# A pre-norm transformer layer on one core: block ends, a tile's place, a layout in memory and the order of the last products

## The chip, the cores and the metric

One core of one Trainium2 chip computes the whole layer in one launch. The metric is the device time of that launch in microseconds. The kernel before was timed three times: 2402.41, 2403.76 and 2404.12 us; the median is 2403.76 us.

## The reference

The input `x` is 2 sequences of 2048 tokens with 1024 features, all in float32. `_layernorm` without gamma and beta is applied ahead of each half.

```python
x = x + attn(layernorm(x))        # one head: d = 256, Wqkv 1024 x 768, Wo 256 x 1024, biases
    # softmax(q k^T / 16) v, then Wo and bo
x = x + ffn(layernorm(x))
    # logits = h @ gate_w (8 experts); s = sum of the two largest logits
    # shared = relu(h @ up_w) ** 2 @ down_w             (1024 -> 2048 -> 1024)
    # routed = ((h @ fc1_w) @ expert_w * s) @ fc2_w     (1024 -> 512 -> 512 -> 1024)
    # layernorm(shared + routed) * ln_gamma + ln_beta
```

The whole routed branch is linear but for the factor `s`, so `expert_w @ fc2_w` (called e2) is formed once, and up with fc1 and down with e2 are two products of inner width 2560.

## The kernel before

**Precision.** Each float32 operand is split into a high part (ScalarE, `A`, line 99) and a low part (VectorE, `TT`, line 102), and each product is three TensorE products (`mm`, line 114): high x high, high x low, low x high.

**Queues.** Every engine runs its instructions in the order in which the program appended them. A wait belongs to the instruction ahead of which it stands, and all behind it on that engine wait as well. DMAs are issued by SP or, for most stores, by ScalarE's queue (`q=act`), and wait there in order too. The order is written out by hand. A `Plan` holds tasks under a number: `plan.add(n, task)` appends what `plan.run(n)` emits behind the products of step n.

**Stage 1, opening.** e2 is computed, x's first tile of 512 tokens is normalised (`ln_stats`, `ln_rstd`, `ln_norm`; the reciprocal root runs on GpSimd) and transposed by TensorE (`xt_tr`) out of `RAW` and split (`xt_evac`).

**Stage 2, q, k and v.** Eight tiles t of 12 steps: eight half groups of q and k, four groups of v. `ev_qk_f` (ScalarE) and `ev_v_f` (VectorE) take the results out of PSUM into a ring of three slots `OUT`; each waits until the slot's last store has landed. Beside it the weights of the FFN are combined, split and stored (`quad_tasks`).

**Stage 3, attention.** Eight blocks i of 512 queries with eight steps k: scores of block i+1 (`pe_S`), product with v of block i (`pe_PV`), and on the other engines subtraction, exponential, high part, sum and low part (`P_sub`, `P_exp`, `P_h`, `P_acc`, `P_l`). At a block's end: `row_sums(i)`, `pe_S(i + 2, 0)`, then `m_tr` (transpose of the running maximum, after `m_fold`), a reduction to `m` on VectorE, `m_bc` (broadcast), and twelve groups `pe_wo` of six products of OH and OL with Wo, whose results `ev_wo` (ScalarE) writes into `ATT` and stores to `att_s`. `pe_wo` used banks 4, 5, 6, 7 in turn.

**LN2.** `ln2_tasks(t, tt)` makes one tile of 128 tokens of the second layernorm: loads, sum to x1, statistics, gate logits, store of x1 + beta (`x1b_s`), normalisation, a transpose in 32 x 32 blocks on VectorE (line 977) and, with the fourth tile, the store of 512 tokens to `xT_s` by 16 DMAs in pieces of 512 B. x1's tiles of t = 1 stood at FFN steps -1, 2, 5 and 8.

**Stage 4, FFN.** Four passes s over 1024 tokens. Both products use a seven-product scheme over 2 x 2 quarters. Up: seven products p in the order 1, 2, 6, 7, 4, 5, 3, ten chunks each; a chunk is 12 products of 512 columns; its moving operand is one of seven combinations B11, B21, T2, T3, T4, T1, B22 of transposed x1, made by `x_sum` and split by `x_piece` into halves. Down: the same order, ten steps each (`d_chunk`, with ring slots filled by `h_op`), results added into quarters A, B (`ZR0`) and D, C (`ZR1`) by `z_evac`; then `z_stat`, `z_fin`, `z_out` and `z_store` make the last layernorm and the residual. A chunk's weights (512 KB) are loaded ahead by `w_fill` from `wu_s` or `wd_s` into six buffers `WR`. Chunks 0 to 6 stand between the steps of the last attention block, chunks 7 to 12 in and ahead of its output groups. In the tail after the last pass, product 3 is done tile by tile and finishes A and B.

Of the kernel before, what the change touches and what calls it, by code (L numbers as in the profile page):

```python
# [69 lines left out]
def transformer_layer(nc, x, wqk, wv, bqk, bv, wo, woT, bo, boc, gate, upfc, dn, expT, fc2, gamma, beta, out):  # L70
# [69 lines left out]
    xT_s = nc.dram_tensor("xT_s", (8, 128, 4096), F32).ap()  # L140
# [249 lines left out]
    ln_norm(0, 1)  # L390
    ln_stats(0, 3)
    ln_rstd(0, 3, 4)
    e2_mm(3, 0)
    f_split(0, 1)
# [6 lines left out]
    f_split(2, 1)  # L401
    xt_tr(0, 0)
# [4 lines left out]
    e2_mm(1, 1)  # L407
# [3 lines left out]
    e2_mm(2, 1)  # L411
# [18 lines left out]
    def out_slot():  # L430
        s = out_n[0] % 3
        out_n[0] += 1
        return s
# [9 lines left out]
    def ev_qk_f(t, i):  # L443
        s = out_slot()
        ev_qk[t, i] = A(OUT[:, s, :], bank(i % 2), AF.Identity, t_pqk[t, i], ld_bq, *out_tok.get(s, ()), bias=bqs[:, i:i + 1])
        out_at[t, i] = s

    def st_qk_f(t, i):
        s = out_at[t, i]
        st_qk[t, i] = dma(qk_s[t, i], OUT[:, s, :], f"out{s}", ev_qk[t, i], q=act)  # L450
        out_tok[s] = (st_qk[t, i],)
# [33 lines left out]
    def kv_load(b, what, k):  # L485
# [8 lines left out]
        else:  # L494
# [3 lines left out]
                                *stg["free"].get(s, ()))  # L498
# [27 lines left out]
    def pe_S(i, k, *toks0):  # L526
        h, lo = QA[i % 2]
        b = i // 4
        for c in range(2):
# [171 lines left out]
    for a in range(4):  # L701
        plan.add(4 + a // 2, xt_tr, 1, a)
        plan.add(4 + a // 2, lambda a=a: xt_evac(1, a, wsp[4], st_e2[0])())
# [60 lines left out]
    T2 = at("T2", [128, 32, 4, 32], F32, 204.71875)  # L764
# [74 lines left out]
    def pe_PV(i, k):  # L839
        b = i // 4  # L840
        h, lo = pslot(i, k)
        for d in range(2):
            o = bank(4 + d)
            for c in range(2):
                kt = 2 * k + c
                toks = [pl_t[i, k], kv_sp[b, "v", k]]
                if k == 0 and i > 0:
                    toks += [att_ev[i - 1, 9]]
# [36 lines left out]

    def pe_wo(i, g):

        tt, c = divmod(g, 3)
        o = bank(4 + g % 4, 344)
# [3 lines left out]
        elif g == 3:  # L893
            prev = rinv_t[i]
        else:
            prev = att_ev[i - 1, 10] if i else wg[1]
        toks = [o_t[i], wo_sp[1], prev]
        for d in range(2):
            mm(o, OH[:, d, ts_], WOH[:, d, ns], d == 0, False, *toks)
            mm(o, OH[:, d, ts_], WOL[:, d, ns], False, False)  # L900
            wo_pe[i, g] = mm(o, OL[:, d, ts_], WOH[:, d, ns], False, d == 1, sig=(d == 1))

    def ev_wo(i, g):
# [5 lines left out]
        att_ev[i, g] = A(ATT[:, n % 2, 344 * c:344 * c + 344], bank(4 + g % 4, 344), AF.Copy, *toks, scale=rinv[:, tt:tt + 1])  # L909
# [774 lines left out]
```

How the kernel before makes its waits and increments, by code:

```python
    def wait(self, *toks):  # L43
        for sem, val in toks:
            if self.known.get(sem.name, 0) < val:
                self.known[sem.name] = val
                self.ops.append(lambda e, s=sem, v=val: e.wait_ge(s, v))
# [1 line left out]
    def put(self, fn, *toks, sig=True):  # L49
        self.wait(*toks)
        if not sig:
            self.ops.append(fn)
            return None
        self.count += 1
        self.ops.append(lambda e: fn(e).then_inc(self.sem, 1))
        return (self.sem, self.count)
# [34 lines left out]
    def dma(dst, src, sl, *toks, q=None):  # L91
        s = slot(sl)
        s.n += 16
        (q or sp).wait(*toks)
        (q or sp).ops.append(lambda e: e.dma_start(dst, src).then_inc(s.sem, 16))
        return (s.sem, s.n)
```

## Time and profile before

| | before |
|---|---|
| median of three runs | 2403.76 us |
| profiled execution | 2404.65 us, its span 2402.8 us |
| TensorE busy | 2330.0 us, 97% of the span, 10888 products |
| VectorE busy | 1577.0 us, 66% |
| ScalarE busy | 790.2 us, 33% |
| GpSimd busy | 284.1 us, 12% |
| mean granted TensorE clock | 0.988 |

A product counts as busy from its start to its modelled end, and one starts before the one ahead has ended; so the pace is read from the number of products in a stretch. PE is TensorE's products, PEld its weight loads, DVE VectorE, ACT ScalarE, POOL GpSimd; SPq and ACTq are the queues that issue DMAs. The times of all rows are microseconds from the span's start unless marked ns.

### The profile page before, as it was taken

How to read it: one execution, taken by the hardware profiler on the slowest of the kernel's cores; microseconds unless marked ns; L12 is line 12 of the kernel's file. 1: busy time of each engine (PE TensorE's matmuls, PEld its weight loads, DVE VectorE, ACT ScalarE, POOL GpSimd, SP SyncE). 2: the span in 40 equal slices, each digit the busy share in tenths (PEclk: the TensorE clock that was granted, in tenths of full speed). 3: DMA queues.
4: the chain of work that ended last, by engine and by line, in shares of the span. 5: the costliest groups of instructions: out<-in, count | busy, mean ns of one | idle time of the engine just before them, and what ended most of it. 6: DMA issues, size and time to landing. Idle time of an engine off the chain costs nothing. (4 is left out here: it accounts for less than half of the span.)

```text
span 2402.8 us, 27319 instructions
## 1 busy us (share of the span) xinstructions
PE 2330.0 (97%) x10888; PEld 1951.2 (81%) x10888; DVE 1577.0 (66%) x1758; ACT 790.2 (33%) x875; POOL 284.1 (12%) x574
## 2 busy tenths in 40 slices
PE   8999999999999889999999999999999999999997
PEld 7989887878888667888888888888888888888885
DVE  7777538888888746478774259876238876434537
ACT  4343325666655432331213132213132121223110
POOL 2101000000031210023210013210003221000002
PEclk9999999999999899999999999999999999999998
DMA  7899624445434587888997678998667999666676
GB/s 292 315 335 363 221 69 137 155 161 193 154 112 135 206 298 252 291 302 288 320 343 240 194 238 272 349 325 280 193 219 266 309 320 330 208 192 195 194 222 201
DMA packets 256895, 581.87 MB, mean 242 GB/s; under 512 B 27520, under 2 KB 114176, under 8 KB 254336
## 3 DMA queue, kind: packets, MB, share of 16 engines
q1 hardware_dynamic: 175392, 444.57, 56.7%
q10 hardware_dynamic: 81376, 135.55, 15.2%
q8 instruction: 86, 1.41, 0.2%
q14 instruction: 41, 0.34, 0.0%
HBM read 424.58 MB, written 155.45 MB: 241 GB/s over the span
## 5 line engine op out<-in xcount | busy, mean ns | idle before, releaser
L102 DVE TENSOR_TENSOR HB<-HB,psum 128x1024 f32<-128x1024 f32 x140 | 169.0, 1217 | 294.1 <-PE psum L114 294.1
L99 ACT ACTIVATE HB<-HB 128x1024 f32<-128x1024 f32 x128 | 135.8, 1061 | 345.4 <-DVE HB L102 343.4
L114 PE MATMUL psum<-XS2h,WR 128*128 128x512 f32 x560 | 176.6, 394 | 13.6 <-issue 10.7
L105 POOL TENSOR_SCALAR veA<-mvA 128x1 f32<-128x1 f32 x32 | 31.1, 971 | 1338.2 <-DVE mvA L191 1338.2
L114 PE MATMUL psum<-XS1h,WR 128*128 128x512 f32 x560 | 176.2, 392 | 3.0 <-DMA WR<-wu_s 3.0
L114 PE MATMUL psum<-XS0h,WR 128*128 128x512 f32 x560 | 175.3, 389 | 0.0
L114 PE MATMUL psum<-XS3h,WR 128*128 128x512 f32 x560 | 174.1, 389 | 0.0
L114 PEld LDWEIGHTS psum<-XS2h,WR 128*128 128x128 f32 x560 | 106.5, 190 | 36.9 <-issue 11.1
L114 PEld LDWEIGHTS psum<-XS1h,WR 128*128 128x128 f32 x560 | 106.0, 189 | 25.9 <-DMA WR<-wu_s 3.8
L114 PEld LDWEIGHTS psum<-XS0h,WR 128*128 128x128 f32 x560 | 105.3, 188 | 21.8
L114 PEld LDWEIGHTS psum<-XS3h,WR 128*128 128x128 f32 x560 | 105.1, 188 | 21.8
L114 PE MATMUL psum<-XS2l,WR 128*128 128x512 f32 x280 | 110.1, 393 | 0.0
L114 PE MATMUL psum<-XS1l,WR 128*128 128x512 f32 x280 | 109.7, 392 | 0.0
L114 PE MATMUL psum<-XS0l,WR 128*128 128x512 f32 x280 | 108.9, 389 | 0.0
L114 PE MATMUL psum<-XS3l,WR 128*128 128x512 f32 x280 | 108.9, 389 | 0.0
L114 PE MATMUL psum<-PH,VH 128*128 128x512 f32 x256 | 101.7, 397 | 3.4 <-DVE PL L102 3.1
L114 PE MATMUL psum<-PL,VH 128*128 128x512 f32 x256 | 100.7, 393 | 0.0
L114 PE MATMUL psum<-PH,VL 128*128 128x512 f32 x256 | 100.6, 393 | 0.0
L102 DVE TENSOR_TENSOR PL<-SA,PH 128x1024 fp32r<-128x1024 f32 x64 | 78.0, 1219 | 29.1 <-ACT PH L99 29.1
L114 PE MATMUL psum<-WR,RG20h 128*128 128x512 f32 x288 | 89.0, 390 | 2.1 <-DMA WR<-wd_s 2.1
L114 PE MATMUL psum<-WR,RG30h 128*128 128x512 f32 x288 | 88.7, 389 | 0.5 <-DMA WR<-wd_s 0.5
L114 PE MATMUL psum<-WR,RG00h 128*128 128x512 f32 x288 | 88.7, 389 | 0.0
(308 smaller groups left out, 5903.4 us busy)
## 6 DMA issues: line engine op xcount, KB each, us to landing
WR<-wu_s SPq DMA_DIRECT2D x280, 512.0 KB, 4.4
WR<-wd_s SPq DMA_DIRECT2D x280, 512.0 KB, 4.8
att_s<-ATT ACTq DMA_DIRECT2D x32, 516.0 KB, 3.0
RAW<-in_x_dram SPq DMA_DIRECT2D x32, 512.0 KB, 8.0
RES<-x1b_s SPq DMA_DIRECT2D x128, 128.0 KB, 5.0
wd_s<-QHc ACTq DMA_DIRECT2D x18, 896.0 KB, 4.8
wd_s<-QRc ACTq DMA_DIRECT2D x18, 896.0 KB, 4.6
HB<-xT_s SPq DMA_DIRECT2D x14, 1024.0 KB, 8.6
```

The source lines that it names most:

```text
L99: return act.put(lambda e: e.activation(o, i, f, **kw), *toks)
L102: return (q or dve).put(lambda e: e.tensor_tensor(o, a, b, op=op), *toks)
L105: return (q or dve).put(lambda e: e.tensor_scalar(o, a, s1, s2, op0=op0, op1=op1), *toks)
L114: return pe.put(lambda e: e.matmul(o, w, m, start=start, stop=stop, **kw), *toks, sig=sig)
```

## The change

The opening's statements are reordered; the transposes of x's second tile stand at plan numbers 5 to 8; the OUT ring has five slots for the first five tiles. At block ends half of the next scores goes behind `m_tr`, `pe_wo` does its OL products last and uses banks 6, 4, 5, 7. Tile (1, 0) of LN2 is begun in block 6; the other three of t = 1 start at 0, 4 and 8; `x_load`, `x_sum` and the pieces that depend on them are two numbers earlier; fewer weight loads are issued in block 6; `row_sums(7)` stands later. `xT_s` has a new layout: a tile is stored by 4 DMAs in pieces of 4 KB, loaded in pieces of 2 KB, and one product reads its 512 columns as four runs of 128. In the last pass the down products run in the order 1, 2, 6, 5, 3, 7, 4, so that A and B are complete first, and the tail finishes C and D.

```diff
@@ opening
+    e2_mm(3, 0)
+    f_split(0, 1)
     ln_stats(0, 3)
     ln_rstd(0, 3, 4)
-    e2_mm(3, 0)
-    f_split(0, 1)
...
     e2_mm(0, 1)
     f_split(2, 1)
+    e2_mm(1, 1)
     xt_tr(0, 0)
...
     f_split(3, 1)
-    e2_mm(1, 1)
+    e2_mm(2, 1)
     wq_split(0)
     xt_tr(0, 2)
     xt_evac(0, 2)()
-    e2_mm(2, 1)
@@ ring
+    outs = [OUT[:, 0, :], OUT[:, 1, :], OUT[:, 2, :], STG[:, 0, :], STG[:, 1, :]]
+
+    def out_slot(t):
+        s = out_n[0] % (5 if t < 5 else 3)
...
     for a in range(4):
-        plan.add(4 + a // 2, xt_tr, 1, a)
+        plan.add(5 + a, xt_tr, 1, a)
@@ block ends
+    def wo_bank(g):
+        return (6, 4, 5, 7)[g % 4]
...
         for d in range(2):
-            mm(o, OH[:, d, ts_], WOH[:, d, ns], d == 0, False, *toks)
+            mm(o, OH[:, d, ts_], WOH[:, d, ns], d == 0, False, oh_t[i], wo_sp[1], prev)
             mm(o, OH[:, d, ts_], WOL[:, d, ns], False, False)
-            wo_pe[i, g] = mm(o, OL[:, d, ts_], WOH[:, d, ns], False, d == 1, sig=(d == 1))
+        for d in range(2):
+            wo_pe[i, g] = mm(o, OL[:, d, ts_], WOH[:, d, ns], False, d == 1, o_t[i], sig=(d == 1))
...
                 if i + 2 < 8:
-                    pe_S(i + 2, 0)
+                    pe_S(i + 2, 0, cs=(0,))
                 m_tr(i + 1)
+                if i + 2 < 8:
+                    pe_S(i + 2, 0, cs=(1,))
                 m_bc(i + 1, sub_t[i, 7])
@@ layout of x1's transposed copy
-    T2 = at("T2", [128, 32, 4, 32], F32, 204.71875)
+    T2 = at("T2", [128, 4, 8, 4, 32], F32, 204.71875)
...
             if tt == 3:
-                for m in range(4):
-                    src = T2[32 * g:32 * g + 32].rearrange("p (j m) t r -> p m j (t r)", m=4)[:, m]
-                    to = xT_s[t, 32 * m:32 * m + 32].rearrange("c (j g q) -> c g j q", g=4, q=128)[:, g]
-                    xt_st[t] = dma(to, src, "xt", ln2_tr[t, 3])
+                src = T2[32 * g:32 * g + 32].rearrange("p m k t r -> p m (k t r)")
+                xt_st[t] = dma(xT_s[t, g].rearrange("(m c) n -> c m n", m=4), src, "xt", ln2_tr[t, 3])
...
-        src = xT_s[2 * s + c, :, 2048 * r:2048 * r + 2048].rearrange("p (j n) -> p j n", j=4)
+        src = xT_s[2 * s + c, :, :, 512 * r:512 * r + 512].rearrange("g p n -> p g n")
...
-            mm(o, w[:, 0, ws], x[0][:, kt, :], kt == 0, False, *toks)
+            mm(o, w[:, 0, ws], x[0][:, :, ws], kt == 0, False, *toks)
@@ attention's end
+    ffn_plan = Plan()
+    x1_tile = ln2_tasks(1, 0, LX, LA, BO, T2, (BETA_A, ld_beta_a), (0, 3))
+    for n, task in zip((53, 53, 61, 61, 61, 61, 65, 65), x1_tile):
+        plan.add(n, task)
+    for n, task in zip((-1, -1, -1, 0), x1_tile[8:12]):
+        ffn_plan.add(n, task)
...
             if i == 6 and g == 0:
                 x_load(0, 0, 0, S_pe_end)
                 x_load(0, 0, 1, S_pe_end)
-                w_fill(0)
-            if i == 6 and g >= 8:
-                x_piece(0, ("B11", "B21")[g // 2 - 4], g % 2)
+            if i == 6 and g == 4:
+                w_fill(-3)
+            if i == 6 and g in (8, 10):
+                x_piece(0, "B11", g // 2 - 4)
+            if i == 6:
+                plan.run(56 + g)
...
-            for tt in range(4):
+            plan.add(-1, w_fill, -1)
+            for tt in range(1, 4):
                 def run(tt=tt):
-                    ln2_at(plan, 3 * tt - 1, LN2_U0, 1, tt, LX, LA, BO, T2, (BETA_A, ld_beta_a), divmod(3 + tt, 4))
-                plan.add(3 * tt - 1, run)
+                    ln2_at(plan, 4 * tt - 4, LN2_U0[tt - 1], 1, tt, LX, LA, BO, T2, (BETA_A, ld_beta_a), (1, tt - 1))
+                plan.add(4 * tt - 4, run)
+            for h in range(2):
+                plan.add(2 + h, x_piece, 0, "B21", h)
...
-                plan.add(14, x_load, 0, 1, r, lambda: (pv_t[7, 7],))
+                plan.add(12, x_load, 0, 1, r, lambda: (pv_t[7, 7],))
...
-                plan.add(16 + n // 2, x_sum, s, name, h)
+                plan.add(14 + n // 2, x_sum, s, name, h)
...
-        if k == 6:
-            row_sums(7)
-            row_inv(7)
     o_evac_h(7)
     o_evac_l(7)
-    for _ in range(2):
-        chunk(nup)
-        nup += 1
+    chunk(nup)
+    row_sums(7)
+    row_inv(7)
+    chunk(nup + 1)
+    nup += 2
@@ last pass
+    PRODS = [(1, 2, 6, 7, 4, 5, 3)] * 3 + [(1, 2, 6, 5, 3, 7, 4)]
...
+        elif s == 3 and p == 6:
+            t = TT(ZD, ZB, src, ALU.add, k, *zt("B"), *free(1))
+            done("D", t)
+        elif s == 3 and p == 5:
+            t = TT(ZC, ZD, src, ALU.add, k, *zt("D"), *free(1))
+            done("C", t)
+        elif s == 3 and p == 3:
+            t = TT(ZB, ZC, src, ALU.add, k, *zt("C"))
+            done("B", t)
+        elif s == 3 and p == 7:
+            done("C", TT(ZC, ZC, src, ALU.add, k, *zt("C")))
+            t = TT(ZD, ZD, src, ALU.add, k, *zt("D"))
+            done("D", t)
...
+    RES = [at(f"RES{i}", [128, 2, 512], F32, o) for i, o in enumerate((168, 172, 0, 4, 8, 12, 16, 20))]
...
+        if s == 3:
+            for tt in range(4):
+                for r in range(2):
+                    plan.add(d + 4 + 8 * tt + 4 * r, lambda r=r, tt=tt: res_load(3, r, tt, up_pe[3, 3, 9]))
+                plan.add(d + 42 + tt, z_stat, 3, 0, tt, 0)
+                plan.add(d + 50 + tt // 2, z_stat, 3, 0, tt, 1)
+                plan.add(d + 52 + 2 * tt, z_out, 3, 0, tt)
+                plan.add(d + 53 + 2 * tt, z_store, 3, 0, tt)
+            plan.add(d + 51, z_fin, 3, 0, 0, 4)
```

## Rows read from the trace of the kernel before

**Rows 1.** The page, section 1: busy us, share of the span, instructions of each engine

```profile
PE 2330.0 (97%) x10888; PEld 1951.2 (81%) x10888; DVE 1577.0 (66%) x1758; ACT 790.2 (33%) x875; POOL 284.1 (12%) x574
```

**Rows 2.** TensorE's waits in the whole run: in total, times, longest

```profile
PE psum L353 <- DVE RAW L105: 8.2, 6, 3.8
PE psum L575 <- DVE m L569: 5.5, 7, 0.8
PE psum L114 <- ACT ATT L99: 4.6, 2, 4.3
PE psum L568 <- DVE mx L102: 3.9, 3, 2.8
PE psum L871 <- DVE acc L102: 3.9, 1, 3.9
PE psum L114 <- DVE OL L102: 3.3, 7, 0.5
PE psum L114 <- DVE PL L102: 3.1, 4, 1.1
PE psum L114 <- DMA WR<-wu_s: 3.0, 2, 2.1
PE psum L114 <- DVE XS2l L102: 2.9, 1, 2.9
PE psum L114 <- DVE F2L L102: 1.9, 2, 1.2
```

**Rows 3.** Stretches: length, busy us (instructions) of each engine, PEclk, DMA share, GB/s

```profile
0.00:60.00 60.00, 52.60 (x254) 43.76 (x255) 42.98 (x66) 26.37 (x34) 17.30 (x50) 0.97 0.80 292
140.00:165.00 25.00, 20.79 (x132) 18.84 (x131) 14.80 (x23) 8.00 (x10) 3.03 (x7) 0.93 0.93 334
780.00:840.00 60.00, 50.04 (x201) 40.13 (x200) 48.21 (x53) 24.32 (x27) 13.99 (x29) 0.89 0.57 212
880.00:910.00 30.00, 14.35 (x46) 10.43 (x46) 21.70 (x22) 5.97 (x7) 0.00 (x0) 0.76 0.61 238
1200.00:1260.00 60.00, 60.00 (x266) 49.56 (x265) 47.83 (x54) 11.01 (x11) 8.51 (x12) 1.00 1.02 344
```

**Rows 4.** VectorE's timeline at 156 us: start, us, engine, line, operation, idle before

```profile
156.61 0.43 DVE L102 TENSOR_TENSOR OUT<-psum,bvb 128x264 f32<-128x264 f32 x1 [5.81 <-DMA qk_s<-OUT]
```

**Rows 5.** Timeline at the end of block 4, VectorE and TensorE

```profile
650.57 0.64 DVE L102 TENSOR_TENSOR mx<-mx 128x512 f32<-128x512 f32 x1
652.68 0.60 PE L568 MATMUL psum<-idn,mx 128*128 128x128 f32 x4
655.19 0.42 PE L114 MATMUL psum<-WOH,OH 128*128 128x344 f32 x1 [0.48 <-DVE OL L102]
```

**Rows 6.** Timeline ahead of the last block, ScalarE and SP's queue

```profile
784.50 0.99 ACT L99 ACTIVATE ATT<-psum,rinv 128x344 f32<-128x344 f32 x2 [4.99 <-DMA att_s<-ATT]
775.62 4.24 SPq L95 DMA_DIRECT2D WR<-wu_s  x5
```

**Rows 7.** Timeline of x1's second half: VectorE, SP's queue, VectorE, TensorE

```profile
859.53 1.25 DVE L977 STREAM_TRANSPOSE T<-LX 128x1024 f32<-128x1024 f32 x1
867.43 7.56 SPq L95 DMA_DIRECT2D xT_s<-T  x8
888.10 1.23 DVE L102 TENSOR_TENSOR HB<-HB,XS0h 128x1024 f32<-128x1024 f32 x1 [10.48 <-DMA HB<-xT_s]
902.41 0.77 PE L114 MATMUL psum<-XS2h,WR 128*128 128x512 f32 x1 [10.71 <-issue]
```

**Rows 8.** Timeline of the tail, TensorE and VectorE

```profile
2385.40 0.39 PE L114 MATMUL psum<-WR,RG30l 128*128 128x512 f32 x1
2380.49 0.67 DVE L102 TENSOR_TENSOR ZR<-ZR,psum 128x512 f32<-128x512 f32 x1
2391.99 0.68 DVE L102 TENSOR_TENSOR ZR<-ZR,psum 128x512 f32<-128x512 f32 x1
2396.94 1.42 DVE L108 SCALAR_TENSOR_TENSOR ZR<-ZR,rZ,RES 128x512 f32<-128x512 f32 x2 [0.69 <-DVE ZR L108]
```

More of the change, by code:

```diff
@@ L443, in ev_qk_f @@
     def ev_qk_f(t, i):
[L444 to L445 removed]
+        s = out_slot(t)
+        ev_qk[t, i] = A(outs[s], bank(i % 2), AF.Identity, t_pqk[t, i], ld_bq, *out_tok.get(s, ()), bias=bqs[:, i:i + 1])
         out_at[t, i] = s
@@ L449, in st_qk_f @@
         s = out_at[t, i]
-        st_qk[t, i] = dma(qk_s[t, i], OUT[:, s, :], f"out{s}", ev_qk[t, i], q=act)
+        st_qk[t, i] = dma(qk_s[t, i], outs[s], f"out{s}", ev_qk[t, i], q=act)
         out_tok[s] = (st_qk[t, i],)
@@ L524, in transformer_layer, with pe_S @@
     MB_t, mxf = {}, {}
-    def pe_S(i, k, *toks0):
+    def pe_S(i, k, *toks0, cs=(0, 1)):
         h, lo = QA[i % 2]
         b = i // 4
-        for c in range(2):
+        for c in cs:
             kt, bk = 2 * k + c, 2 * (k % 2) + c
@@ L1571, in transformer_layer @@
         if g == 11:
-            bank_free.update({4 + b: (att_ev[7, 8 + b],) for b in range(4)})
+            bank_free.update({wo_bank(n): (att_ev[7, n],) for n in range(8, 12)})
         if g % 3 == 2:
@@ L1589, in transformer_layer, with tail_out1, tail_out2 @@
     for tt in range(4):
-        res_load(3, 0, tt)
-    for tt in range(4):
-        z_stat(3, 0, tt, 0)
+        z_stat(3, 1, tt, 1)
     mul = {}
-    def tail_out1(tt):
-        for c in range(2):
-            z, cs = ZR[0][:, c, tt, :], slice(512 * c, 512 * c + 512)
-            mul[tt] = STT(z, z, mvZ[:, tt, 0:1], GAMMA[:, cs], ALU.subtract, ALU.mult, ag_t[3, 0, tt])
-    def tail_out2(tt):
-        for c in range(2):
-            z, cs = ZR[0][:, c, tt, :], slice(512 * c, 512 * c + 512)
-            k = STT(z, z, rZ[:, tt:tt + 1], RES[tt][:, c, :], ALU.mult, ALU.add, mul[tt], fin[3, 0, tt], res_ld[3, 0, tt])
-            for ps, rs in parts(3, 0, tt):
-                dma(out[rs, cs], ZR[0][ps, c, tt, :], f"zo{tt}{c}", k, q=(act, sp)[c])
+    def tail_out1(tt, c):
+        z, cs = ZR[1][:, c, tt, :], slice(512 * c, 512 * c + 512)
+        mul[tt] = STT(z, z, mvZ[:, tt, 0:1], GAMMA[:, cs], ALU.subtract, ALU.mult, ag_t[3, 1, tt])
+    def tail_out2(tt, c):
+        z, cs = ZR[1][:, c, tt, :], slice(512 * c, 512 * c + 512)
+        k = STT(z, z, rZ[:, tt:tt + 1], RES[4 + tt][:, c, :], ALU.mult, ALU.add, mul[tt], fin[3, 1, tt], res_ld[3, 1, tt])
+        for ps, rs in parts(3, 1, tt):
+            dma(out[rs, cs], ZR[1][ps, c, tt, :], f"zo{tt}{c}", k, q=(act, sp)[c])
     done = {}
```

127 lines of the change are left out of this document (63 added, 64 removed).

## The prediction

> **What bounds the kernel now.** I began with the page's busy shares: TensorE is busy 97% of the span [rows 1], and no part of the change takes away a matrix product. So the change can only take away time in which TensorE stands or runs slowly. I looked for that time in two views: TensorE's waits over the whole run [rows 2], and stretches of time with TensorE's count of products and its granted clock [rows 3]. The last row of rows 3 gives the pace when nothing is in the way: 266 products of 512 columns in 60 us, 0.226 us each. The others show what is lost. From 880 to 910 us only 46 products start, 10.4 us of work in 30 us: 19.6 us are lost in one place. From 780 to 840 the mean clock is 0.89; 0.11 below full is 0.22 of the 60 us at 1.2 instead of 2.4 GHz, 13 us that do half their work: 6.6 us lost beside the waits. The same arithmetic gives 3.6 us at 1.2 GHz (1.8 us lost) in 0 to 60 and 3.5 us (1.7 lost) in 140 to 165. The waits of rows 2, the late start of the second x1 half and the end of the run are the whole field: about 80 us, most of it between 780 and 910 us, where the attention ends and the FFN begins.
>
> The profiled execution lasted 2404.65 us (span 2402.8). The sum below is made against 2404.65; the median of the runs is 0.9 us less.
>
> **1. Opening: orders of a few statements.** `f_split(0, 1)` now stands ahead of the statistics of tile 3, so TensorE's 1.2 us for F2L goes (the larger of two, 1.9 in all [rows 2]). `e2_mm(1, 1)` ahead of the first transposes puts 12 products (2.7 us) before the wait for the normalised RAW, but that normalisation gets 0.7 us later. The transposes of tile row 1 move one to three chunks later (plan 4, 4, 5, 5 to 5, 6, 7, 8), behind 2.7 us of products. RAW costs 8.2 us in all, of which 3.8 belong to part 2; of the other 4.4 I take 2.8, and half of the 1.8 us of clock: 1.2 + 2.8 + 0.9 = 4.9 us. What is late next: `pe_v(0, 2)` waits for the evacuation of the last transpose with one product group of cover; I price that at nothing and keep 1 us in the range.
>
> **2. OUT ring of five.** At 156.6 VectorE waited 5.81 us for a store of `qk_s` before it could reuse an OUT slot [rows 4]. Queued behind it are two normalisations, and TensorE's transposes wait for those: 3.8 us, the longest wait for RAW, and 1.7 us of clock [rows 2, 3]. With five slots for t < 5 the slot in question was stored two evacuations earlier. The two extra slots are the staging buffers, first loaded for other use at plan 67, behind the last stores. Gain 5.5 us.
>
> **3. Block ends.** At seven ends TensorE transposes the running maximum, waits 0.8 for its reduction (m), broadcasts it, and waits 0.5 for OL (5.5 and 3.3 us over seven [rows 2]). Now half of the next scores (6 products, 1.36 us) stands between the transpose and the broadcast, and the first output group does its four OH products before it needs OL; its bank order 6, 4, 5, 7 lets it start while banks 4 and 5 are still read. From the transpose to the output product it took 655.19 - 652.68 = 2.51 us [rows 5]; two groups of four small transposes (0.44 each, as far as the second starts behind the first, an estimate from their 0.60) and the moved 1.36 make 2.24, of which 1.36 is work that was elsewhere: 0.88 against 2.51, 1.6 us saved. That needs the folded maximum 1.36 us sooner. At 652.68 it had been ready since 651.21, 1.47 us before: enough, and this is the smallest slack of four ends (the others have 1.8 to 3.0). At two ends TensorE was waiting for the fold (mx) itself (three waits, 3.9 us, the longest 2.8 [rows 2]; the third is ahead of the first block); there the moved half only lengthens that wait, and 0.3 us is left (2.51 less 2.24). The last end has no next scores: only OL, 0.5. Sum 4 x 1.6 + 2 x 0.3 + 0.5 = 7.5 us. VectorE's own work per block doesn't shrink, so I subtract 0.5 for P parts that come later relative to TensorE: 7.0.
>
> **4. Before the last block.** ScalarE waited 4.99 us for `att_s<-ATT`, TensorE 4.3 of the 4.6 for ATT [rows 2, 6]. The store was in flight together with 2 MB of x1 and five 512 KB weight loads issued from 775.6 [rows 6]. Now there are two of those, and the x1 loads are issued earlier: 4 issues instead of 16 write x1's transposed copy ahead of them. The wait goes; of the 6.6 us of clock [rows 3] half hangs on it, the other half on part 5. 4.3 + 3.3 = 7.6, less 1.2 because `x_piece` and the early tile now stand in ScalarE's and VectorE's queues there: 6.4 us.
>
> **5. Last block.** `row_sums(7)` goes behind `o_evac_l(7)` and one more chunk, 8 us later: the 3.9 us for acc and its 3.3 us of clock go, 7.0 us, since the inverse is needed only at output group 3, after another chunk. Against it: LN2 tile (1, 0) is added in the output products of block 6, and tiles 1 to 3 follow every 4 chunks. I laid VectorE's queue beside TensorE's, at 1.2 us per operation of 1024 elements [rows 7]: 17 operations for the block's subtractions, sums and low parts, 2 for the end of tile (1, 0), 6.5 for each of two tiles, 2 for B21, 34 operations or 41 us. TensorE has 15 groups of 12 products, 41 us: no slack. PL waits were 3.1 us [rows 2]; I expect about 1 us more. Net 6.0.
>
> **6. x1's second half.** The chain of before: the last LN2 tile is transposed at 859.5 to 860.8; SP issues the copy in 16 transfers (eight of them from 867.43, ending at 875.0); VectorE gets B12 at 888.1 after 10.48 us of idling; TensorE starts product 6 at 902.4 after 10.71 us [rows 7], then waits 2.9 more [rows 2]. 27.3 us from transpose to data, 14.3 from data to product. TensorE was ready at 902.4 - 10.7 = 891.7, and without the weight wait of 2.1 [rows 2] and 1.7 us of clock just before it would have been at 887.9. Now: the transpose comes about 1 us earlier relative to chunk 8 (its `att_s` load still waits for the store of the tile before it). The 2 MB copy, at the 344 GB/s of a full stretch [rows 3], is 6 us, with issue and landing 8; the load is at plan 12 instead of 14, so ahead of gamma's and beta's loads: 1 MB is 3.0 us at the same rate, with the 4.4 us that the last output took to land [rows 8] about 7. So 15 instead of 27.3 us: data at 859.8 + 15 = 874.8. VectorE reaches the sums, now at plan 14, at chunk 14's end, five chunks (13.6 us) before product 6 is due: 874.3. The 14.3 us stay: sums T1, T2, T4 and the first piece, all on VectorE in the same order. Product 6 has its data at 889.1, 1.2 us late. I take 1.5 us, the 2.9 for XS2l's second half unchanged and 2 us of clock: 6.4 of the 19.6 us stay, 13.2 go.
>
> Per group of four tiles SP spends 16 issues on the copy, eight of them 7.56 us [rows 7]; I lean on the issues, not on the piece size. The Trainium skill's page DMA: Bandwidth & Descriptors, section Specifications, sets the smallest transfer for line rate at 512 B; by that rule the larger pieces buy no transfer time. That result is rival B below. No run here shows the rule by itself.
>
> Reads of x1 now come in 2 KB instead of 8 KB pieces. Bounds: nothing, or another 3.0 us for a load of 1 MB; only the two of part 6 are without cover.
>
> **7. x1 as moving operand.** 280 chunks x 12 = 3360 products now read 512 columns as four runs of 128, a kind of read that no row shows. Below: 0 (a gain is excluded, since 0.226 us is also the pace with contiguous columns). Above: four transposes of 128 columns take 0.60 us [rows 5] against 0.226, +0.37 us each, some 1200 us. I take 0, the row with the same number of columns per instruction. The splits read strips of 256 with the same element count: 0 as well.
>
> **8. The end.** Before, TensorE ended at 2385.79, but VectorE began the first of four last tiles only at 2380.5, being busy with the other half's outputs; the last tile took from 2391.99 to 2398.36, 6.4 us, and everything was over 4.4 us later [rows 8]. With the order 1, 2, 6, 5, 3, 7, 4 the half A, B is complete two products earlier and its outputs lie beside products. A tile takes TensorE 18 products, 4.1 us, and VectorE 17.9 / 4 = 4.5 with its waits: it keeps up. The last tile then starts at about 2385.9 and ends at 2392.3: 6.1 us saved. The eight RES loads, 32 issues in four groups, pass SP with the weight loads: 0 to 1 us of weight wait.
>
> **Sum:** 4.9 + 5.5 + 7.0 + 6.4 + 6.0 + 13.2 + 6.1 = 49.1 us. 2404.65 - 49.1 = 2355.6; against the median 2354.7.
>
> **Rivals.**
> A. VectorE becomes the bound around the last block: it loses an operation's length or two at each of eight steps (8 x 1.2 us), the tiles slip, and with them part 6 by the same amount up to 5. For it: the balance of part 5 has no slack. Against: before, with two tiles, PL cost 3.1 us in all. 2355 + 10 + 3 = 2368.
> B. The copy of x1 isn't ready sooner: the landing, not the issues, set 875 to 888, and the larger pieces change no transfer. Then only the 2 chunks of earlier load (5.4 us) help and product 6 still waits about 5 us more, with its clock: 2355 + 7 = 2362.
> C. Better: block ends and B12 come out whole, the clock stays up: 1.5 + 2 + 1.2 + 1.8 us: 2348.
> D. Slower than before: the four-run read of part 7. It decides from 49.1 / 3360 = 0.015 us per product, 7% of the pace; at a tenth of the upper bound, 0.037, it is +124 us: 2479. Nothing in the profile speaks for it but that no row excludes it.
>
> **How the numbers follow.** Forecast 0.57, A 0.18, B 0.12, C 0.09, D 0.04. The time is the forecast's, 2354.7. The range takes in C and A and their bounds: 2342 to 2374. A measurement of this kernel can tell about 0.2% (5 us) from no change. Faster: all but D and a stray 0.02: 0.94; same 0.02; slower 0.04.
>
> **What would show it.** The page's chunks: 266 products in 60 us must stay (D). The wait for ATT and for acc absent (4, 5). m and OL absent at five ends, and the fold's wait longer at block 2 (3). VectorE's wait for `qk_s<-OUT` at 150 to 157 gone (2). Product 6 starts with under 3 us of wait; if B12's wait on VectorE is still 5 us or more, B. PL waits above 6 us would be A. The last output on VectorE ends 6 to 7 us after TensorE's last product, not 12.6 (8). The forecast is wrong if the 780 to 910 stretch gives back less than 15 us.

## The result, and the profile after

| | before | after |
|---|---|---|
| median | 2403.09 us (4 runs) | 2361.09 us (4 runs, 2359.59 to 2363.95) |
| profiled execution | 2404.65 us, span 2402.8 | 2361.47 us, span 2359.7 |
| mean granted TensorE clock | 0.988 | 0.994 |
| TensorE busy | 2330.0 us | 2318.3 us |

The ratio is 0.9826, 95% interval 0.9809 to 0.9843: 42 us gained, where 49.1 were forecast (2354.7 us; 2361.09 is inside the range). The spans differ by 43.1 us. The first part of the page of after answers to [rows 1]:

```profile
span 2359.7 us, 27222 instructions
PE 2318.3 (98%) x10888; PEld 1945.5 (82%) x10888; DVE 1576.2 (67%) x1758; ACT 788.8 (33%) x875; POOL 291.8 (12%) x574
```

TensorE's largest waits of after stand against [rows 2] (in total, times, longest):

```profile
PE psum L114 <- ACT ATT L99: 7.7, 7, 2.2
PE psum L570 <- DVE mx L102: 6.3, 4, 4.1
PE psum L114 <- DMA WR<-wu_s: 5.4, 3, 3.7
PE psum L114 <- DVE XS2l L102: 3.4, 1, 3.4
PE psum L114 <- DVE XA1l L102: 1.2, 1, 1.2
PE psum L114 <- DMA WR<-wd_s: 1.0, 1, 1.0
PE psum L114 <- DVE F2L L102: 0.9, 1, 0.9
PE psum L577 <- DVE m L571: 0.8, 1, 0.8
PE psum L114 <- DVE PL L102: 0.6, 1, 0.6
```

The waits for RAW (8.2), acc (3.9) and OL (3.3) are gone, m fell from 5.5 to 0.8, PL from 3.1 to 0.6. Three of those of before grew: ATT from 4.6 to 7.7, mx from 3.9 to 6.3, weights from 3.0 to 5.4. The same kinds of stretches as in [rows 3], moved to where the work now stands (columns as there):

```profile
0.00:60.00 60.00, 57.58 (x287) 48.40 (x288) 46.42 (x72) 26.80 (x34) 18.66 (x54) 1.00 0.81 301
140.00:165.00 25.00, 25.00 (x141) 21.69 (x140) 16.65 (x26) 8.39 (x10) 0.00 (x0) 1.00 1.05 399
745.00:805.00 60.00, 54.89 (x268) 46.74 (x268) 53.16 (x58) 31.03 (x38) 18.33 (x26) 1.00 0.73 250
845.00:875.00 30.00, 22.94 (x81) 17.89 (x81) 23.11 (x20) 9.54 (x10) 0.00 (x0) 0.80 0.76 274
1200.00:1260.00 60.00, 60.00 (x268) 49.67 (x268) 40.45 (x40) 21.92 (x22) 4.68 (x6) 1.00 0.91 294
```

The last row is the pace: 268 products in 60 us against 266. The two rows hold different products (161 of the 266 are down products, which read no x1), so the stronger evidence is one stretch of equal work: from the first to the last up product of the second pass it takes 191.11 us in before and in after. Four runs of 128 columns cost nothing. Three stretches are at full clock now. The row of 845 to 875 shows what is left: 81 products in 30 us, at a mean clock of 0.80.

I followed the gain by the start of the same product in both traces, as the timelines give it (us; the last column is what the stretch brought):

| product | before | after | in this stretch |
|---|---|---|---|
| first scores (parts 1, 2) | 327.72 | 316.46 | 11.25 |
| first output product of block 6 (part 3) | 771.08 | 752.72 | 7.10 |
| chunk 0 (part 4) | 794.85 | 774.57 | 1.92 |
| chunk 7 (part 5) | 840.28 | 809.93 | 10.07 |
| chunk 17 | 879.27 | 850.83 | -1.91 |
| chunk 21 (part 6) | 910.03 | 873.33 | 8.25 |
| last product | 2385.40 | 2347.68 | 1.03 |
| from there to the end | 17.4 | 12.0 | 5.4 |

These are single executions, and two things in them move from one to the next. Two kernels below whose opening is that of before start the first scores at 325.91 and 329.57 us. And in the 22 us around the end of block 5 the mean granted clock was 0.92 in before, in last_order_alone and in no_4k_layout, and 1.00 in ring_alone, in block_ends_alone and in after, which is worth about 2 us. So a difference of under 2 us between two traces is no proof, unless a wait in them shows it.

### The profile page after: what moved, and what is told of

The parts are those of the page before. It is cut to its first block, busy times and chain, and to the rows that moved or that the text cites. A ratio compares the mean times of both kernels' runs of the same rounds, so it can differ in the third digit from the quotient of the medians.

```text
span 2359.7 us, 27222 instructions
## 1 busy us (share of the span) xinstructions
PE 2318.3 (98%) x10888; PEld 1945.5 (82%) x10888; DVE 1576.2 (67%) x1758; ACT 788.8 (33%) x875; POOL 291.8 (12%) x574
## 4 chain that ended last, share of the span: by engine, by line
PE 81%; DVE 7%; DMA 7%; ACT 3%; issue 1%; POOL 1%; SPq 0%; ACTq 0%; DVEq 0%; POOLq 0%
PE psum L114 80%; DMA wu_s<-QR0a 2%; DMA QR0a<-in_upfc_dram 1%; DMA wd_s<-QRc 1%; DVE mx L102 1%; PE psum L353 1%; ACT SA L99 1%; DVE QR0a L102 1%; DVE HB L102 1%; DVE QRc L102 1%; DMA att_s<-ATT 1%; DVE acc L102 1%; ACT ATT L99 1%; DVE st L188 1%; DMA WR<-wu_s 1%
## 5 line engine op out<-in xcount | busy, mean ns | idle before, releaser
L114 PE MATMUL psum<-WR,RG10h 128*128 128x512 f32 x288 | 88.7, 389 | 0.0
```

The lines of the kernel that those rows point to most:

```text
L114: return pe.put(lambda e: e.matmul(o, w, m, start=start, stop=stop, **kw), *toks, sig=sig)
```

## Experiments

Each time is a median of one study's runs. Chips and hours move the kernel before from 2399.8 to 2404.2 us, so between studies the ratios to it are compared, and inside a trace the starts of products. Diffs are excerpts; `...` stands for lines left out.

**ring_alone.** The kernel before with the ring of five slots alone:

```diff
-    def out_slot():
-        s = out_n[0] % 3
+    outs = [OUT[:, 0, :], OUT[:, 1, :], OUT[:, 2, :], STG[:, 0, :], STG[:, 1, :]]
+
+    def out_slot(t):
+        s = out_n[0] % (5 if t < 5 else 3)
...
```

> The kernel before with the OUT ring of five alone. Theory (store wait): the 5.8 us wait of VectorE for a qk_s store at 150 to 157 us goes and with it TensorE's 3.8 us wait for RAW and 1.7 us of clock: 5 to 6 us less, and nothing else moves. Rival (the opening and the ring share the gain of 9.3 us that the changed kernel has at the first scores beyond the 2.0 of the opening): the ring alone gives clearly more or less than 5.5, outside 4.5 to 6.5.

2394.68 us, ratio 0.9971 (0.9961 to 0.9981): 7 us, above the 5 to 6 expected; the interval reaches down to 4.6. The first scores start 5.4 us sooner, and VectorE's wait for `qk_s<-OUT` of [rows 4] is gone. The trace's other 1.5 us lie at the end of block 5, where this trace has no dip of the clock; the ring has no part in that. Part 2 holds.

**last_order_alone.** The kernel before with the last pass in the new order and with the new tail:

```diff
-    SEQ_D = [(p, kt) for p in (1, 2, 6, 7, 4, 5, 3) for kt in range(10)]
+    PRODS = [(1, 2, 6, 7, 4, 5, 3)] * 3 + [(1, 2, 6, 5, 3, 7, 4)]
+    SEQ_D = [[(p, kt) for p in PRODS[s] for kt in range(10)] for s in range(4)]
...
```

> The kernel before with the last pass's order of down products, its eight RES buffers and the new tail alone. Theory: TensorE's end stays within 1 us, the last output follows TensorE's last product by 6 to 7 us instead of 12.6: 5 to 6.5 us less. Rival: the changed kernel gained another 1.6 us inside the last pass before the tail; if that belongs to this part (fewer weight waits there), the whole is 6.5 to 7.5 us less.

2396.72 us, ratio 0.9981 (0.9971 to 0.9990): 4.6 us, just under the 5 to 6.5 expected, which the interval covers. From the last product to the end it takes 11.6 us instead of 17.4. Part 8 holds.

**block_ends_alone.** The kernel before with the split scores, OL last and the bank order:

```diff
                 if k == 0 and i > 0:
-                    toks += [att_ev[i - 1, 9]]
+                    toks += [att_ev[i - 1, 10]]
...
+    def wo_bank(g):
+        return (6, 4, 5, 7)[g % 4]
...
-                    pe_S(i + 2, 0)
+                    pe_S(i + 2, 0, cs=(0,))
                 m_tr(i + 1)
+                if i + 2 < 8:
+                    pe_S(i + 2, 0, cs=(1,))
...
```

> The kernel before with the block ends alone (half of the scores behind the transpose of the maximum, OL products last, banks 6 4 5 7). Theory: 1.6 us less at the ends of blocks 0, 1, 3, 4, about 0.3 at 2 and 5, 0.5 at 6: 7 us less. Rival (as the changed kernel showed at block 2, where it lost 1.5 us): an end where the fold is late costs time, since the halved clock that follows the longer idle falls on products: 5 us less in all, with block 2 at +1 or worse.

2391.53 us, ratio 0.9957 (0.9941 to 0.9973): 10.3 us, where 7 were expected; the interval covers that. Block 6's first output product starts 9.9 us sooner, but 1.8 of these are there at the first scores already, which this edit does not touch: 8.1 belong to the blocks. By the output products, time is lost at block 2 alone (1.06 us): TensorE waits there for the fold, as in after. Two waits for ScalarE's evictions are new in this kernel, and in after too; before has none at these places:

```profile
779.48 0.76 PE L114 MATMUL psum<-PH,VH 128*128 128x512 f32 x1 [2.13 <-ACT ATT L99]
853.01 0.47 PE L114 MATMUL psum<-XS1h,WR 128*128 128x512 f32 x1 [1.17 <-ACT ATT L99]
```

**no_4k_layout.** The changed kernel with the old layout of `xT_s` (16 stores in pieces of 512 B, one contiguous moving operand), all else as changed:

```diff
-                src = T2[32 * g:32 * g + 32].rearrange("p m k t r -> p m (k t r)")
-                xt_st[t] = dma(xT_s[t, g].rearrange("(m c) n -> c m n", m=4), src, "xt", ln2_tr[t, 3])
+                for m in range(4):
+                    src = T2[32 * g:32 * g + 32].rearrange("p (j m) t r -> p m j (t r)", m=4)[:, m]
+                    to = xT_s[t, 32 * m:32 * m + 32].rearrange("c (j g q) -> c g j q", g=4, q=128)[:, g]
+                    xt_st[t] = dma(to, src, "xt", ln2_tr[t, 3])
...
```

> The changed kernel with the layout of x1's transposed copy undone: 16 stores per four tiles in 512 B pieces, loads in 8 KB pieces, moving operands contiguous. Theory of the prediction (issues set the copy's time): the copy of the second half takes 5 us longer or more, product 6 is later by as much: +5 to +10 us. Rival (the copy's rate is set by something that both layouts share; before, copy and load took 16.7 us to landing, now 14): only about 3 us at that place, +1 to +4 us in all. If reading four runs of 128 cost TensorE anything, this kernel would be faster than that by it; expected 0.

2368.56 us, ratio 0.9861 (0.9841 to 0.9881): by the ratios the layout is worth 8.4 us of the 42; the two intervals just overlap. The traces differ by 8.7 us, and only 2.3 of these lie between chunk 17 and chunk 21, where the layout was to help. Another 2.4 lie between block 6's first output product and chunk 0, where TensorE waits once, 5.34 us, in place of twice, 2.23 and 2.10; about 2 are the clock at the end of block 5. Two lines of SP's queue, first of no_4k_layout, then of after (start, duration of the issues):

```profile
834.52 13.61 SPq L95 DMA_DIRECT2D xT_s<-T  x16
850.50 0.80 SPq L95 DMA_DIRECT2D HB<-xT_s  x2
```

```profile
830.66 4.47 SPq L95 DMA_DIRECT2D xT_s<-T  x4
844.61 0.93 SPq L95 DMA_DIRECT2D HB<-xT_s  x2
```

The issues shrank by 9.1 us, but the time from the first issue to the load, which waits for the landing, only from 16.0 to 14.0 us. Over that time the DMA engines moved 245 GB/s in pieces of 512 B and 249 in pieces of 4 KB. The up products of the second pass take the same 191.11 us in both.

**no_copy_wait.** The changed kernel; in the first pass x1's second half is loaded from the copy of t = 0, which landed long ago. The sums work on other data, the rest is the same.

```diff
+        t = 0 if s == 0 else 2 * s + c
+        src = xT_s[t, :, :, 512 * r:512 * r + 512].rearrange("g p n -> p g n")
+        x_ld[s, c, r] = dma(raw, src, f"x{c}{r}", xt_st[t], *free())
```

> The changed kernel, with x1's second half of the first pass loaded from the copy of the first half (t = 0), which landed long ago; so the first pass works on other numbers there, and nothing waits for the copy of t = 1. Theory (the copy's 14 us to landing holds SP's queue, so weights, and the sums): the loads issue 7 us or more earlier, weight wait 3.7 goes, sums start at chunk 14's end, product 6 starts 6 to 8 us earlier; the 3.4 for the second half of XS2l stays. Rival (the sums' own length binds): product 6 at most 2 us earlier.

2363.16 us (two runs), ratio 0.9846 (0.9826 to 0.9865): no gain. Now the loads are issued while the copy is still under way:

```profile
832.65 5.79 SPq L95 DMA_DIRECT2D xT_s<-T  x4
841.11 5.56 SPq L95 DMA_DIRECT2D HB<-xT_s  x2
```

VectorE gets B12 in it, and in after:

```profile
854.05 1.23 DVE L102 TENSOR_TENSOR HB<-HB,XS0h 128x1024 f32<-128x1024 f32 x1 [7.52 <-DMA HB<-xT_s]
```

```profile
850.82 1.23 DVE L102 TENSOR_TENSOR HB<-HB,XS0h 128x1024 f32<-128x1024 f32 x1 [7.08 <-DMA HB<-xT_s]
```

Counted from the copy's first issue, that is 21.4 us against 20.2. The wait for the copy's landing costs nothing by itself: what was issued sooner landed no sooner. The DMA engines were full all that time (a mean share of 1.00, and 0.97 in after). That their work and not the order of issue sets the arrival is the reading that fits; direct_copy below tries it.

**copy_128_partitions.** The changed kernel with a third layout: the tile is stored by one DMA that reads all 128 partitions, and loaded in four pieces of 32 partitions each.

```diff
-            if tt == 3:
-                src = T2[32 * g:32 * g + 32].rearrange("p m k t r -> p m (k t r)")
+            if tt == 3 and g == 0:
+                src = T2[:, :, :, :, :].rearrange("p m k t r -> p m (k t r)")
...
+        for m in range(4):
+            src = xT_s[2 * s + c, :, m, 512 * r:512 * r + 512].rearrange("(g c) n -> c g n", g=4)
+            x_ld[s, c, r] = dma(raw[32 * m:32 * m + 32], src, f"x{c}{r}", xt_st[2 * s + c], *free())
```

> The changed kernel with the copy of four tiles stored by one DMA from all 128 partitions (16 KB runs), and loaded by four DMAs of 32 partitions for each half. Theory (a transfer that touches 32 partitions runs at about half the rate, 180 to 200 GB/s, as the copy does in the changed kernel): the copy lands in 6 to 9 us instead of 14, the first load takes about as long as now plus 2 to 3 us: B12 is there 3 to 5 us earlier and product 6 likewise; in passes 1 to 3 nothing. 2 to 5 us less in all. Rival (the rate is set by DRAM writes or by the load beside it): the copy still takes 12 us or more and the kernel is slower by the slower loads.

2385.34 us, ratio 0.9932 (0.9907 to 0.9956): 24 us slower than after (25 by the ratios). Its copy is the fast one. The last two columns are the DMA engines' busy share and GB/s, first from the copy's issue to the load's, then from there to B12; in after and then here:

```profile
830.66:844.61 13.95, 12.78 (x63) 10.83 (x62) 2.77 (x4) 4.27 (x6) 0.27 (x1) 1.00 0.97 249
844.61:850.82 6.21, 6.21 (x31) 5.14 (x30) 0.00 (x0) 1.28 (x2) 0.00 (x0) 1.00 0.97 338
```

```profile
833.69:842.60 8.91, 7.74 (x40) 6.69 (x39) 1.55 (x3) 3.43 (x5) 0.29 (x1) 1.00 0.99 373
842.60:850.90 8.30, 8.30 (x39) 6.86 (x38) 1.22 (x1) 2.12 (x2) 0.00 (x0) 1.00 0.99 260
```

The engines are full in all four rows, and the figures are of everything in flight. Beside stores that read 32 partitions each they moved 249 GB/s, beside the one that reads 128 it was 373; beside the wide load 338, beside the narrow loads 260. From issue to the load it takes 8.9 us instead of 14.0, and B12 is there after 17.2 us instead of 20.2. In the first pass that pays as expected: from chunk 17 to chunk 21 it takes 18.47 us here and 22.50 in after, 4.0 less. The loss comes behind it. The narrow transfers are now the loads, 64 of them, in all four passes, and the down weights come late:

```profile
PE psum L114 <- DMA WR<-wd_s: 18.4, 10, 4.2
```

The Trainium skill tells of the width on its page SBUF — State Buffer, section "Door 1: The DMA port swizzle": a transfer's rate follows how many of the 16 ports its partitions reach, and 32 neighbouring partitions reach half of them. The trace agrees in direction, 249 against 373 GB/s with other transfers beside them in both. Its section "Can I just issue two DMAs to hit both halves?" says that two narrow transfers don't add up; with four in flight here all traffic together stayed at 249 GB/s, which agrees too.

This layout for the tile of the first pass alone was not tried.

**direct_copy.** The changed kernel; tile t = 1 goes from SBUF straight into the buffers that the sums read, with no copy in DRAM for this tile:

```diff
+                if t == 1:
+                    to = quarters(0)[2][:, 0:4].rearrange("p (r a) b n -> p r (a b) n", r=2)
+                    for m in range(4):
+                        xt_st[t] = dma(to[32 * m:32 * m + 32, :, g], src[:, m].rearrange("p (r n) -> p r n", r=2), "xt", ln2_tr[t, 3], pv_t[7, 7])
+                    x_ld[0, 1, 0] = x_ld[0, 1, 1] = xt_st[t]
+                    return
...
-            for r in range(2):
-                plan.add(12, x_load, 0, 1, r, lambda: (pv_t[7, 7],))
```

> The changed kernel with one thing moved: the transposed tile t = 1 goes from SBUF straight into the two SBUF buffers that product 6's sums read (16 stores of 128 KB on SP's queue), and is not written to DRAM and read back. Theory (what the DMA engines have to move after the transpose sets when B12 is there, not the wait for the copy's landing, which no_copy_wait took away without gain): the 2 MB that were read back are gone, the 16 issues take 13.6 us as the 16 of no_4k_layout did, so the first sum starts 2 to 4 us sooner than 20.2 us after the transposition's end (850.82 less 830.6), product 6's wait falls by as much, and the time is 2357 to 2360 against 2361.1. Rival (the chain of sums and ScalarE's copy behind it, or the weights, hold product 6 whatever B12 does): 2361 or more. Rival (16 issues hold SP's queue and with it the weights): a weight wait above 3.8 us at chunk 18, 2362 to 2365.

2358.34 us, ratio 0.9815 (0.9795 to 0.9835). SP's and VectorE's lines:

```profile
830.27 12.24 SPq L95 DMA_DIRECT2D HB<-T  x16
```

```profile
844.85 1.23 DVE L102 TENSOR_TENSOR HB<-HB,XS0h 128x1024 f32<-128x1024 f32 x1 [1.31 <-DMA HB<-T]
```

B12 is there 14.6 us after the first issue instead of 20.2, the weight wait at chunk 18 is gone, and chunk 21 starts at 867.35 instead of 873.33, from nearly the same start of chunk 17 (850.63 against 850.83). Taking 2 MB off the engines moved the data where taking away the wait did not. The expectation had 2 to 4 us; the trace shows 6.0. That execution took 2353.37 us and was the shortest of its four (to 2360.55); by the ratios the gain over after is 2.6 us, and the two intervals overlap. Inside its own study it is 5.5 us under second_load_later, which comes out as a kernel like after.

**weights_held.** The changed kernel; the five weight loads in block 6 wait until that block's second ATT store has landed; to be in the queue behind it, the first of them move from group 4 to group 6:

```diff
+        if c < 5:
+            toks.append(att_st[6, 1])
...
-            if i == 6 and g == 4:
+            if i == 6 and g == 6:
                 w_fill(-3)
```

> The changed kernel with the weight loads of chunks 0 to 4 held until the second ATT store of block 6 has landed. Theory (they share the DMA engines with that store; five are issued at 757.6 to 761.1, not two): ScalarE's wait for att_s<-ATT 2.9 falls under 1.5, TensorE's two waits for ATT (2.2 and 2.1) fall by 2 to 3 us in all. Rival (the 2 MB of x1 alone delay the store): the waits change by less than 1 us.

2361.99 us, ratio 0.9839 (0.9823 to 0.9856): no difference. The store that ScalarE needs was issued at 758.19 and landed at 765.8: 7.6 us, where it took 7.2 in after, with no weight load near it. The weights are not what it stood behind.

**second_load_later.** The changed kernel with the load of B21 and the weights moved from the first and the fifth group of block 6's output product to the seventh:

```diff
+            if i == 6 and g == 6:
                 x_load(0, 0, 1, S_pe_end)
-            if i == 6 and g == 4:
                 w_fill(-3)
```

> The changed kernel with the load of x1's second quarter (B21, 1 MB) and the five weight loads behind it issued after order 6 of block 6's output product instead of after orders 0 and 4. Theory: the ATT store issued at 756.96 took 7.2 us because it stood behind 2 MB of x1's first half, since weights_held moved the weights alone and the store still took 7.6; with 1 MB less ahead of it (3 us at 340 GB/s) ScalarE's wait of 2.94 us falls to under 1, TensorE's two ATT waits of 2.23 and 2.10 us to under 2.5 together, and the time is 2358 to 2359.5. Rival (a store of ATT takes 7 us in this stretch whatever is ahead of it, since the earlier LX, LA and copy traffic fills the engines): the two waits stay above 4 us, 2361.

2363.88 us, ratio 0.9834 (0.9817 to 0.9851), and no answer. The load was issued at 757.35, no later than in after (756.60), since SP's queue stood in the wait for the copy until 756.9 anyway. The edit moved a line in the program and nothing in time.

**early_fold.** The changed kernel with `m_fold` right behind the last subtraction's maximum instead of a step later:

```diff
                 mx_op(i + 1, k + 1)
+                if k == 6:
+                    m_fold(i + 1)
             else:
-                m_fold(i + 1)
```

> The changed kernel with m_fold one step sooner (right behind the last maximum), ahead of the plan's tasks of step 6 in VectorE's queue, where at block 2 the sums of a down half wait 2.75 us for their DMA. Theory (what was lost at blocks 2 and 5 is the fold's place): the waits for mx, 6.3 us, go but for 0.5, with the halved clock at 518: 6 to 9 us less. Rival (VectorE has no room, the time comes back as waits for PL or m): under 3 us less.

2355.49 us, ratio 0.9815 (0.9800 to 0.9830). By the ratios that is 2.6 us under after, and the intervals overlap; inside its own study it is 6.5 us under weights_held, which made no difference to after, and its trace is 5.7 us shorter than that of after. VectorE at block 2, in after and then here:

```profile
518.16 1.55 DVE L102 TENSOR_TENSOR QRc<-QRc 128x256 f32<-128x256 f32 x4 [2.75 <-DMA QRc<-in_dn_dram]
519.63 0.69 DVE L102 TENSOR_TENSOR mx<-mx 128x512 f32<-128x512 f32 x1
```

```profile
515.07 0.69 DVE L102 TENSOR_TENSOR mx<-mx 128x512 f32<-128x512 f32 x1
515.68 0.68 DVE L102 TENSOR_TENSOR KL<-KVR,KH 128x512 fp32r<-128x512 f32 x1
518.24 1.55 DVE L102 TENSOR_TENSOR QRc<-QRc 128x256 f32<-128x256 f32 x4 [1.88 <-DMA QRc<-in_dn_dram]
```

In after the fold of 0.69 us stood in VectorE's queue behind an operation of the weights' preparation that waited 2.75 us for a DMA. TensorE's waits for mx fall from 6.3 us to 0.2, those for m rise from 0.8 to 3.6, and the output product of block 2 starts 3.7 us sooner, that of block 5, all blocks to there together, 5.5.

**fold_direct_later.** The changed kernel with the edits of early_fold, direct_copy and second_load_later, whose diffs stand above.

> The changed kernel with three edits together: early_fold's (2355.5 by itself), direct_copy's and second_load_later's. If each keeps its worth, 2355.5 less 2 to 3 less 2 to 2.5: 2350 to 2352. If the stretch around the last block has one bound that all three share, 2354 to 2356.

2351.50 us, ratio 0.9784 (0.9767 to 0.9801): 10 us under after by the ratios, and clear of its interval. Inside the study it is 12.4 us under second_load_later, where direct_copy is 5.5; with early_fold's 6.5 the two gains about add up.

**second_load_held.** fold_direct_later with one wait more, which does move the load in time:

```diff
-                x_load(0, 0, 1, S_pe_end)
+                x_load(0, 0, 1, lambda: (S_pe[7, 7], att_st[6, 1]))
```

> fold_direct_later with one wait added: the load of B21 (1 MB) and, behind it on SP's queue, the five weight loads wait until the second ATT store of block 6 has landed. In second_load_later and fold_direct_later the load was only moved in the queue, where the wait for the copy's landing held it anyway (issued 757.35 there and 756.60 in the changed kernel, 750.96 in fold_direct_later), so that nothing was moved in time. Theory: the store of ATT (issued 751.43 in fold_direct_later, 7.3 us to landing, where the median of these stores is 4.3) stands behind x1's loads; with one of the two gone it lands 2.5 to 3 us sooner, TensorE's waits of 2.85 and 1.84 us there fall to under 2.5 together, and the time falls by 2 to 3 us, to 2348.5 to 2349.5 against 2351.5. Rival 1: the B11 load alone fills the engines as long as the store needs; the waits stay above 4 us, and the time is 2351 to 2352. Rival 2: the weights come late, since they are issued only when the store has landed: a new weight wait at chunk 0 of 1 us or more, 2352 to 2355.

2348.95 us, ratio 0.9786 (0.9773 to 0.9800). ScalarE in fold_direct_later, then here (the store, and the write that needs its slot):

```profile
751.43 0.33 ACTq L95 DMA_DIRECT2D att_s<-ATT  x1
759.11 0.99 ACT L99 ACTIVATE ATT<-psum,rinv 128x344 f32<-128x344 f32 x2 [3.42 <-DMA att_s<-ATT]
```

```profile
751.40 0.33 ACTq L95 DMA_DIRECT2D att_s<-ATT  x1
757.97 0.99 ACT L99 ACTIVATE ATT<-psum,rinv 128x344 f32<-128x344 f32 x2 [2.30 <-DMA att_s<-ATT]
```

TensorE, here:

```profile
758.57 0.42 PE L114 MATMUL psum<-WOH,OH 128*128 128x344 f32 x1 [1.57 <-ACT ATT L99]
762.84 0.66 PE L114 MATMUL psum<-PH,VH 128*128 128x512 f32 x1 [2.12 <-ACT ATT L99]
```

The store lands 1.1 us sooner, the first wait is half, the second as before, and chunk 0 starts 1.4 us sooner. So of the wait for ATT the load of B21 is 1.1 to 1.4 us, not 3 (the weight loads behind it moved too, which weights_held showed to be worth nothing); both kernels have the same ratio to before, so this edit's worth is below what these runs can tell. The best version is one of these two, 2.1 to 2.2% under the kernel before.

## Why the prediction was right, part by part

The measured 2361.09 us is inside the range of 2342 to 2374, but 6.4 us above the forecast of 2354.7 and within a microsecond of the 2362 of rival B, and B's own sign is there: VectorE waited 7.08 us for B12, where 5 or more was to mean B. The gain as a whole, its places and most of its sizes are those of the forecast: from block 6's first output product to chunk 21 it is 18.3 us, where under 15 would have refuted it. Parts 4 and 6 fell short by 9.4 us, and parts 1, 2, 5 and 8 brought more than was said.

**Parts 1 and 2 (10.4 forecast, 11.25 measured).** ring_alone gives 5.4 at the first scores for part 2 (5.5 forecast), which leaves 5.9 for part 1 (4.9); both are good to about 2 us, since the untouched opening moves by that. No clock was lost in either window.

**Part 3 (7.0, measured 7.1).** The total is right by two errors, and that is luck. Where the fold was ready (blocks 0, 1, 3 and 4) the ends gave what was said, 1.3 to 1.7 us each. At block 2 I left 0.3 us of gain; there 1.5 us were lost by its output product, because a moved fold-dependent transpose waited 4.1 us, and 0.8 more behind it. At block 5 I left 0.3 too, and 2.4 came; ring_alone, which has no edit there, gains 2.0 at the same place: the clock dips to 0.92 there in before and not in these two. I had read the slack of the fold at the ends where it was there, not what stood ahead of it on VectorE at the two where it was late. early_fold shows the cause and that it could be had.

**Part 4 (6.4, measured 1.9).** This is the step that failed. "The wait goes" rested on fewer weights in flight and an earlier load of x1. There were five weight loads again, not two (`w_fill(-3)` and the fill at step -1 come in one stretch, because the latter waits for nothing), and x1's loads could be issued only when the copy had landed:

```profile
744.41 5.18 SPq L95 DMA_DIRECT2D xT_s<-T  x4
756.18 0.38 SPq L95 DMA_DIRECT2D XS0r<-xT_s  x1
757.64 3.47 SPq L95 DMA_DIRECT2D WR<-wu_s  x5
```

11.8 us from issue to landing puts them right ahead of the ATT store of 756.96, as before. TensorE waits 2.23 and 2.10 us. weights_held shows that the five weight loads are not the cause and second_load_held that x1's second load is a quarter to a third of it. The second wait came with part 3's edit: block_ends_alone, with the x1 loads and the weights where before has them, waits 2.13 us at the same product. In its diff that product, the next block's first with v, waits for the eviction of group 10 in place of group 9, since the new bank order puts group 10 into bank 5. Part 3 had counted that order as a gain and put its price at nothing. What holds the rest of the first wait stays open. The clock did come back: 1.00 in 745 to 805.

**Part 5 (6.0, measured 10.1).** 0.4 of the 10.1 only moved: the four products of `row_sums(7)` now stand behind chunk 7's start and count in the next row of the table. The acc wait went, and PL fell to 0.6 us instead of growing by 1. Rival A is refuted. Its size and mine came from 1.2 us per VectorE operation of 1024 elements; back to back they start 1.13 to 1.15 us apart (504.10 to 505.24 in block 2), so 34 operations are 39 us, not 41. In 745 to 805 VectorE is busy 53.16 of 60 us. That part 5's edit alone brought these 10.1 us is not shown. Parts 4 and 5 together brought 12.0 from block 6's first output product to chunk 7, and block_ends_alone, which has neither edit, brings 3.8 there: its wait for acc is 2.8 us instead of 3.9, and the 20 us around chunk 6 run at a mean clock of 1.00 (810 to 830) instead of 0.83 (820 to 840 in before).

**Part 6 (13.2, measured 8.25, less the 1.9 lost just ahead).** I put 8 us on the copy and 7 on the load, 15 in all. It took 14.0 and 6.2: 20.2 us. The copy is the term that was mis-sized. 344 GB/s was the rate of a full stretch made mostly of weight loads over 128 partitions, and this one reads 32 at a time among weight loads, two stores of ATT and an x1b store; rows 3's rate was not its rate. Rival B came true in the main: as it said, the issues did not set the arrival (13.6 us to 4.5, worth 2.0), and the larger pieces changed no rate (245 and 249 GB/s). What it didn't say is what sets the landing. The wait for it is worth nothing (no_copy_wait); the engines' time is what counts, as a wider store (copy_128_partitions) and fewer bytes (direct_copy) both show. From data to product it took 14.9 us (14.3 forecast). And one wait is new:

```profile
857.50 0.80 PE L114 MATMUL psum<-XS1h,WR 128*128 128x512 f32 x1 [3.67 <-DMA WR<-wu_s]
870.61 0.80 PE L114 MATMUL psum<-XS2h,WR 128*128 128x512 f32 x1 [3.39 <-DVE XS2l L102]
```

The x1 load stands in SP's queue until 844.61, and the weight loads behind it start only at 847.02, after gamma and beta. I had written that a weight wait of 2.1 would go; it became 3.7. Product 6 then starts without a wait of its own at 865.70, 0.7 us after its data (863.82 + 1.22). direct_copy removes the weight wait, and the product starts 0.1 us after its data (857.84 + 1.22, start 859.16). So without the weight wait product 6 of after would have started at most 0.7 us sooner: the data is the bound, and the weight wait hid it. The rest is clock: 30 us less 81 products at 0.226 and less these two waits leaves 4.6 us, where I had left 2. Of the 1.9 us lost just ahead, 0.4 are the moved row sums, and 1.17 are one more wait that part 3's edit brought, for ScalarE's ATT at 836.79, behind the last output product, as in block_ends_alone.

**Part 7 (0).** The up products of the second pass take 191.11 us in before, after and no_4k_layout. Rival D is refuted.

**Part 8 (6.1, measured 5.4 behind the last product, and 1.0 more between chunk 21 and it).** VectorE ends 7.0 us after TensorE's last product starts, 6.6 after it ends (6 to 7 forecast):

```profile
2347.68 0.39 PE L114 MATMUL psum<-WR,RG30l 128*128 128x512 f32 x1
2353.27 1.42 DVE L108 SCALAR_TENSOR_TENSOR ZR<-ZR,rZ,RES 128x512 f32<-128x512 f32 x2 [0.69 <-DVE ZR L108]
```

By their ratios, the four parts tried alone gain 7.0, 4.6, 10.3 and 8.4 us, 30 of the 42. The opening (part 1), the earlier LN2 tiles and loads, and the later `row_sums(7)` were not run alone.

## What to carry to other kernels

Price a transfer by the rate of its own shape and by what is already queued on the engines; taking away its issues, or the wait ahead of it, moved little or nothing here while the engines were full, and taking away bytes did. Before a short operation on the critical path is counted as ready, read what stands ahead of it in its queue, above all anything that waits for a DMA. When banks are given out in a new order, list what waits for each bank's last reader: the price can stand in another stretch than the gain. A line moved in a queue that is standing in a wait moves nothing in time: move it with a wait, and look at its time of issue.

## What the runs showed of the hardware

With the DMA engines full (share 0.97 to 0.99), all traffic together was 249 GB/s during stores that read 32 partitions each and 373 during one that reads 128; 260 during narrow loads and 338 during wide ones. Turning the copy round for all tiles doesn't help: the narrow loads then cost 18.4 us of weight waits over the run. 16 stores from SBUF to SBUF were issued in 12.24 us and brought 2 MB in 14.6 us, where the way through DRAM took 20.2. A moving operand of four runs of 128 columns went at the pace of 512 contiguous ones, 191.11 us for the same stretch of products. The mean granted clock around one and the same block end was 0.92 in some of these kernels and 1.00 in others, with and without an edit there: about 2 us that belong to no edit.
